# Transposing one input of a channel cross-attention on VectorE instead of TensorE, on one Trainium2 core

## What is computed

```python
rgb, geo = x transposed to (b, n, c), ctx transposed to (b, n, c)
def xca(q, k, v):                       # attention over channels, not positions
    attn = softmax(einsum('bhni,bhnj->bhij', q, k) * scale)
    return einsum('bhnd,bhde->bhne', v, attn)
res_p2r = xca(rgb @ wq_rgb.T, geo @ wk_point.T, geo @ wv_point.T) @ proj_p2r.T
res_r2p = xca(geo @ wq_point.T, rgb @ wk_rgb.T, rgb @ wv_rgb.T) @ proj_r2p.T
out = transpose(rgb + res_p2r) + transpose(geo + res_r2p)
```

## Time and profile before

| | |
|---|---|
| runs of the kernel before | 145.23, 145.45, 145.67 us (median 145.45) |
| profiled execution, span | 144.7 us (no time of its own is given beside the three runs) |
| TensorE matmul busy | 135.4 us, 94% |
| VectorE busy | 99.1 us, 68% |
| ScalarE busy | 92.6 us, 64% |
| GpSimd busy | 2.0 us, 1% |
| DMA | 25.80 MB, mean 178 GB/s |
| mean granted clock of TensorE | 0.985 |

### The profile page before, as it was taken

How to read it: one execution, slowest core, us unless ns; L and a number is a source line. 1 busy time by engine, 2 the same in 40 slices (tenths; PEclk the granted TensorE clock), 3 DMA queues, 4 the chain that set the end, 5 groups by cost and what they waited for, 6 DMA issues and landing times. The chain is left out here.

```text
span 144.7 us, 3130 instructions
## 1 busy us (share of the span) xinstructions
PE 135.4 (94%) x968; PEld 123.4 (85%) x968; DVE 99.1 (68%) x245; ACT 92.6 (64%) x207; POOL 2.0 (1%) x11
## 2 busy tenths in 40 slices
PE   7599889999999999999999999999999999997871
PEld 7399778999999998999999998989999998986560
DVE  0125797678686977777786878777785969777740
ACT  3125948675766767785876767686867677582821
POOL 5000000000000000000000000000000000000000
PEclk9959999999999999999999999999999999999998
DMA  4999243431919467482828475583927730303033
GB/s 132 246 418 417 96 140 150 147 147 31 348 61 248 191 183 249 142 289 60 296 86 263 172 239 196 165 270 89 310 53 245 317 147 0 145 0 150 2 147 145
DMA packets 7642, 25.80 MB, mean 178 GB/s; under 512 B 849, under 2 KB 977, under 8 KB 7633
## 3 DMA queue, kind: packets, MB, share of 16 engines
q1 hardware_dynamic: 7632, 25.69, 52.2%
HBM read 17.30 MB, written 8.39 MB: 178 GB/s over the span
## 5 line engine op out<-in xcount | busy, mean ns | idle before, releaser
L383 DVE COPY gt<-gt_ps 128x512 f32<-128x512 f32 x32 | 22.1, 691 | 18.1 <-PE gt_ps L228 18.1
L238 PE MATMUL gu_ps<-gt,xt 128*128 128x128 f32 x256 | 34.5, 281 | 0.0
L238 PEld LDWEIGHTS gu_ps<-gt,xt 128*128 128x128 f32 x256 | 33.2, 198 | 1.2
L372 ACT COPY out_sb<-out_ps 128x512 f32<-128x512 f32 x32 | 17.7, 587 | 18.0 <-DMA out_dram<-out_sb 11.0
L387 DVE TENSOR_TENSOR x_lo<-x_raw,x_hi 128x1024 fp32r<-128x1024 f32 x16 | 19.6, 1226 | 4.1 <-ACT x_hi L327 4.1
L318 ACT COPY xt<-xt_ps 128x512 f32<-128x512 f32 x32 | 18.9, 589 | 5.0 <-PE xt_ps L228 4.9
L354 ACT ACTIVATE expd<-scores,min_neg 128x128 f32<-128x128 f32 x32 | 12.6, 395 | 12.8 <-DVE min_neg L427 12.8
L228 PE MATMUL xt_ps<-ident,x_raw 128*128 128x128 f32 x128 | 19.3, 273 | 1.1 <-DMA x_raw<-in_x_dram 1.1
L228 PE MATMUL gt_ps<-ident,g_raw 128*128 128x128 f32 x128 | 19.8, 278 | 0.6 <-DMA g_raw<-in_ctx_dram 0.6
L387 DVE TENSOR_TENSOR g_lo<-g_raw,g_hi 128x1024 fp32r<-128x1024 f32 x16 | 19.5, 1216 | 0.0
L228 PEld LDWEIGHTS xt_ps<-ident,x_raw 128*128 128x128 f32 x128 | 15.4, 142 | 3.2 <-DMA x_raw<-in_x_dram 1.3
(11 more groups left out here) (51 smaller groups left out, 193.1 us busy)
## 6 DMA issues: line engine op xcount, KB each, us to landing
x_raw<-in_x_dram SPq DMA_DIRECT2D x15, 512.0 KB, 3.5
g_raw<-in_ctx_dram SPq DMA_DIRECT2D x15, 512.0 KB, 5.3
out_dram<-out_sb SPq DMA_DIRECT2D x15, 512.0 KB, 5.9
x_raw<-in_x_dram SPq DMA_DIRECT2D x2, 256.0 KB, 3.8
g_raw<-in_ctx_dram SPq DMA_DIRECT2D x2, 256.0 KB, 4.4
out_dram<-out_sb SPq DMA_DIRECT2D x2, 256.0 KB, 2.0
w_sb<-in_weights_dram SPq DMA_DIRECT2D x1, 384.0 KB, 7.1
w_sb<-in_weights_dram SPq DMA_DIRECT2D x1, 128.0 KB, 5.0
```

The source lines that it names most:

```text
L238: last = nc.tensor.matmul(gram_ps, xt[:, cols], gt[:, cols], start=(t == 0), stop=(t == TILES - 1))
L372: nc.scalar.copy(out_sb[:, slot % OUT_SLOTS, cols], out_ps[:, cols]).then_inc(half_copied, 1)
L383: nc.vector.tensor_copy(gt[:, cols], gt_ps[:, cols]).then_inc(gt_copied, 1)
```

## The change

- **G is loaded twice.** Beside the plain `g_raw`, a second copy `gz` is loaded with quarters of the channels and of the positions exchanged: `gz[32 q + k, 256 a + m]` is channel 32 a + k at position 256 q + m. It comes in pieces of 1 KB, by four DMAs of 32 partitions each, for two batches at a time; SP issues quarters 0 and 1, ScalarE quarters 2 and 3.
- **VectorE transposes G** in blocks of 32x32 from `gz` straight into `gt` (`turn_half`, two instructions of 128x512 a batch). TensorE no longer transposes G, and `gt_ps` goes.
- **X stays on TensorE**, in chunks of every eighth column, so that its positions stand in the same order as G's. `xt_ps` shrinks to one half; VectorE makes both copies of it, into a double buffer.
- **Low parts on GpSimd.** `x_lo` and `g_lo` are made by GpSimd, not VectorE.
- s, exp, y and t have a PSUM bank each; the exponentials are written to PSUM, t gets the identity added in place, probs is one instruction in place of two.
- **One more stage.** Transposes run in step i, the gram matrix in i+1, the small products with t in i+2, the last product in i+3, its second output copy in i+4. All steps are written out, with no loop. Four output slots in place of two, 56 warm-up matmuls in place of 24, `ident2` made directly.

The core of the diff: the turned load, then in this order GpSimd's loop, SP's, TensorE's transposes, ScalarE's loop and VectorE's turn.

```diff
-WARM = 24
+WARM = 56
+        g_turn = ctx.rearrange("b (a k) (q m) -> q k (b a) m", a=QUADS, q=QUADS)
+        def load_turned(eng, src, dst, done, first, count, quads):
+            pair, at = first // 2 % PAIRS, first % 2
+            for q in quads:
+                into = dst[q * QUAD:(q + 1) * QUAD, pair, at:at + count, :]
+                eng.dma_start(into.rearrange("p e (a m) -> p (e a) m", a=QUADS),
+                              src[q][:, QUADS * first:QUADS * (first + count), :]).then_inc(done, 16)
...
+            for b in range(B):
+                split_lo(b, x_raw, x_hi, x_lo, x_hi_ready)
+                split_lo(b, g_raw, g_hi, g_lo, g_hi_ready)
...
+            for i in range(2, B + 4):
+                if i % 2 == 0 and i + 2 < B:
+                    sp.wait_ge(gt_turned, 2 * i)
+                    load_turned(sp, g_turn, gz, gz_loaded[(i + 2) // 2 % PAIRS], i + 2, 2, (0, 1))
+                if 0 <= i - 4 < B - 1:
+                    store(i - 4)
+                if i >= 3 and i + 1 < B:
+                    sp.wait_ge(xt_done, 2 * (i - 3) + 2)
+                    sp.wait_ge(lo_ready, 2 * (i - 3) + 2)
+                    load_plain(i + 1)
...
+            def transpose_half(b, half):
+                slot = b % SLOTS
+                pe.wait_ge(x_loaded[slot], 16 * (b // SLOTS) + 16)
+                if 2 * b + half >= 1:
+                    pe.wait_ge(xt_copied, 2 * b + half)
+                blocks = x_raw[:, slot, :].rearrange("p (n j) -> p j n", j=TILES)
+                for t in range(TILES // 2):
+                    last = nc.tensor.transpose(xt_ps[:, t * TILE:(t + 1) * TILE], blocks[:, half * TILES // 2 + t, :],
+                                               ident[:, :])
+                last.then_inc(xt_done, 1)
...
+            for i in range(1, B + 4):
+                g, s, l, e = i - 1, i - 2, i - 3, i - 4
...
+                if i % 2 == 0 and i + 2 < B:
+                    act.wait_ge(gt_turned, 2 * i)
+                    load_turned(act, g_turn, gz, gz_loaded[(i + 2) // 2 % PAIRS], i + 2, 2, (2, 3))
+                if out_on:
+                    evacuate(e, 1)
+                if small_on:
+                    act.wait_ge(uv_done, s + 1)
...
+            def turn_half(b, half):
...
+                if b >= 2:
+                    dve.wait_ge(gram_done, b - 1)
+                blocks = gz[:, pair, b % 2, :].rearrange("p (a i j) -> p j a i", a=QUADS, i=QUAD)
+                first = half * TILES // 2
+                cols = slice(half * HALF, (half + 1) * HALF)
+                nc.vector.transpose(gt[:, b % 2, cols].rearrange("p (j a k) -> p j a k", a=QUADS, k=QUAD),
+                                    blocks[:, first:first + TILES // 2, :, :]).then_inc(gt_turned, 1)
```

More of the change, by code:

```diff
@@ L187, in _ @@
[L187 to L191, removed]
+                sp.dma_start(out[b], out_sb[:, b % OUT_SLOTS, :]).then_inc(out_stored[b % OUT_SLOTS], 16)
@@ L195, in _ @@
+            sp.dma_start(g_raw[:, 1, :], ctx[1]).then_inc(g_loaded[1], 16)
             for b in range(2, SLOTS):
[L196 to L199, removed]
+                load_plain(b)
+            for i in range(2, B + 4):
[8 more added lines that the diff above has]
+                    load_plain(i + 1)
@@ L215, in _ @@
                 nc.tensor.matmul(out_ps[:, 0:P], warm[:, :], warm[:, :], start=True, stop=True)
[L216 to L222, removed]
-                if i_min >= 1:
-                    pe.wait_ge(copied, 2 * i - 1 + half)
+            pe.wait_ge(ident_ready, 3)
@@ L239, in gram_half, with last_parts @@
                 if half == 1:
                     last.then_inc(gram_done, 1)
-            def last_half(b, slot, half, b_min):
+            def last_parts(b, half, first, end):
+                slot = b % SLOTS
                 cols = slice(half * HALF, (half + 1) * HALF)
-                if b_min >= 1:
-                    pe.wait_ge(half_copied, 2 * b - 1 + half)
                 parts = [(t_hi, 0, x_hi), (t_hi, 0, x_lo), (t_hi, 1, g_hi), (t_hi, 1, g_lo), (t_lo, 0, x_hi), (t_lo, 1, g_hi)]
-                for n, (w, which, moving) in enumerate(parts):
+                if first == 0 and b >= 1:
+                    pe.wait_ge(half_copied, 2 * (b - 1) + 1 + half)
+                for n in range(first, end):
+                    w, which, moving = parts[n]
@@ L248, in last_half @@
                     if half == 0 and n == 4:
                         pe.wait_ge(t_lo_ready, b + 1)
-                    last = nc.tensor.matmul(out_ps[:, cols], w[:, which, :], moving[:, slot, cols],
-                                            start=(n == 0), stop=(n == len(parts) - 1))
-                last.then_inc(half_done, 1)
-            def step(i, slot, visit, i_min):
-                gram_on, small_on, last_on = i_min < B, 1 <= i_min <= B, i_min >= 2
-                before = (slot - 2) % SLOTS
-                if gram_on:
-                    turn(i, visit, i_min, 0, x_raw, slot, x_first_loaded, x_loaded, xt_ps, xt_done, xt_copied)
-                    turn(i, visit, i_min, 0, g_raw, slot, g_first_loaded, g_loaded, gt_ps, gt_done, gt_copied)
+                    last = nc.tensor.matmul(out_ps[:, cols], w[:, which, :], moving[:, slot, cols], start=(n == 0),
+                                            stop=(n == len(parts) - 1))
@@ L260, in step @@
+                if end == len(parts):
+                    last.then_inc(half_done, 1)
+            for i in range(B + 3):
+                g, s, l = i - 1, i - 2, i - 3
+                turn_on, gram_on, small_on, last_on = i < B, 0 <= g < B, 0 <= s < B, 0 <= l < B
                 if small_on:
-                    pe.wait_ge(gram_lo_ready, i)
-                    if i_min == 1:
+                    pe.wait_ge(gram_lo_ready, s + 1)
+                    if s == 0:
                         pe.wait_ge(wu_lo_ready, 1)
@@ L306, in step @@
                 if last_on:
-                    last_half(i - 2, before, 1, i_min - 2)
-            steps(pe, step, 0, B + 1)
+                    last_parts(l, 1, 2, 6)
+                if small_on:
+                    pe.wait_ge(y_copied, s + 1)
+                    if s >= 1:
+                        pe.wait_ge(t_lo_ready, s)
+                    nc.tensor.matmul(t_ps[:, 0:P], y_sb[:, 1, :], w_sb[:, PR, :], start=True, stop=True)
+                    nc.tensor.matmul(t_ps[:, P:2 * P], y_sb[:, 0, :], w_sb[:, PP, :], start=True,
+                                     stop=True).then_inc(t_done, 1)
```

348 lines of the change are left out of this document (164 added, 184 removed).

## The result

| | before | changed |
|---|---|---|
| runs, median (us) | 145.56 (145.23 to 146.64, 4 runs) | 158.06 (157.44 to 159.18, 4 runs) |
| ratio, 95% interval | | 1.0835, 1.0777 to 1.0893 |
| profiled span (us) | 144.7 | 156.7 |
| first uv, second uv start (us) | 11.92, 17.71 | 17.33, 29.94 |
| from second uv to span's end (us) | 127.0 | 126.8 |

The change makes the kernel 8% slower; the forecast of 145.2 us was wrong, and so was the range, which ended at 153. The last row of the table says where to look: everything from the second batch's uv on takes as long as before (14 steps are 1.1 us longer, the end behind the last uv is 1.3 us shorter), and the whole loss, 12.2 us, lies in front of it.

The account below looks back on a forecast made before the run. TensorE's list of work was taken to set the step. 13.5 + 6.9 + 100.1 + 3.75 + 7.15 + 5.6 + 7.5 gave a 144.5 us span, plus 0.75 the forecast 145.2, no change; range 139.5 to 153.

Parts of the forecast that it names:

- Head and tail: Start and end of the kernel: uv of batch 0 at 13.5 us, 6.9 for step 2, 7.15, 5.6 and 7.5 for steps 16 to 18.
- Rival D: X loads at even steps: X lands 1.2 us late in six steps behind turned G and a store, 152 us; chance 0.13.
- TensorE's work: TensorE's step of 8.09 us: G's transposes go, 0.83 us a batch, leaving 7.26; 13.3 us could be gained over 16 batches.
- rival B: X's transposes on TensorE: strided weight loads take double, 0.42 us more per four, +8 to 153.2 us; chance 0.13.
- rival A: ScalarE's issues do not hold it, 140.7 us; with the step's gaps of 0.51 hidden as well, 134; chance 0.30.
- Wait 1: TensorE's s waits for ScalarE's uv copy, starting 1.20 us after uv instead of 0.87: gap of 0.31 us a step.
- wait 2: TensorE's y waits for probs, behind VectorE's second X copy: gap of 0.25 us a step.
- Wait 3: ScalarE at even steps: two DMA issues, taken at 0.75 us, delay the uv copy, so s starts 0.75 us later.
- Rival C: VectorE's turn reads at half rate because of the stride, 0.53 us longer each, 149 us; chance 0.10.
- What is hidden: VectorE's step falls to 5.1 of 7.7 us; GpSimd's subtractions, 1.6 to 3.2 us each, are costed at nothing.
- Tail: End of the kernel: step 16 takes 7.15 us, step 17 5.6 and step 18, to the span's end, 7.5.

Follow-up runs that it names:

- the last version: Changed kernel with TensorE's G for batches 0 and 1, X and G first, later ScalarE issues, s behind first gram half, t behind next uv: 136.59 us.

## Why the prediction was wrong

Its own sum against the profile, in us of span:

| term | forecast | measured |
|---|---|---|
| uv of batch 0 | 13.5 | 17.33 |
| step 2, to uv of batch 1 | 6.9 | 12.61 |
| 13 full steps | 103.85 | 106.7 |
| step 16 to the end | 20.25 | 20.07 |
| span | 144.5 | 156.7 |

**The step that failed is "Head and tail": 13.5 and 6.9.** Both were summed from TensorE's and VectorE's instructions, with every tile in place when wanted. When X of batches 1 and 2 would land was never asked, though all of it was at hand: SP's order in the kernel, the sizes, and 330 GB/s in the start. By those, 4.5 MB ahead and 0.5 MB of its own would have put X of batch 2 at 15 us or later, past the 14.0 us at which its transposes were to begin (13.5 and uv's 0.45). That names the wait, but only the first 1 to 2 of its 8 us: the trace shows 22.40, for the rate was 290, hardly a byte moved in the first 2 us, and 5.8 MB had moved by the landing (257 GB/s over 22.4 us), so that later loads shared the rate. 9.5 of the 12.2 us missed lie here, and the earlier landing in one experiment, the shorter queue in another, gave 3.9 and 6.4 us back (156.7 to 152.8 and 150.3). Of the first two rows of the table only the sum holds from one execution to the next. Uv of batch 0 is late by X of batch 1 (2.18 us of waiting) and by gram halves at half clock behind that wait (1.91 us in place of 1.06); in the runs that leave the start's loads alone it comes at 14.4 to 17.3 us, and uv of batch 1 at 28.0 to 29.9 all the same, since X of batch 2 lands at 20.8 to 22.5.

**Rival D was the right mechanism in the wrong place.** It was worked out for even steps, where the changed kernel shows no wait for X: its slow steps cover the late load. Freed of ScalarE's issues, the kernel shows it at once (five waits of 1.1 to 2.5 us in odd steps); and its remedy is the order alone, since 277 to 308 GB/s were carried with X on time. That the pieces of 1 KB cost rate is not excluded: the start ran at 286 to 294 GB/s against 330 before, and at 338 (3 to 14 us) in the run that loads no turned G for batches 0 and 1, but no run tells their size from the other differences there.

**TensorE's work was right.** 7.26 us of work in a step; 7.22 in the last version. Four transposes of strided X take 0.45 from start to start (92.86 to 93.31) where four took 0.40 to 0.44, so a strided load costs 0.01 us at most and not 0.11, and B was to count from 0.03 on: **rival B is false.** (Their weight loads are recorded as 0.19 us long, 0.14 before; the contiguous loads of the gram matrix are 0.19 as well, and only the distance of starts tells a cost.) Of rival A one figure does not follow: its hidden gaps are 0.56 by waits 1 and 2, or 0.44 by the step of 7.7, and not 0.51.

**Wait 1 and wait 2 were right.** s starts 1.07 us after uv in odd steps (1.20 forecast), and an odd step takes 7.75 (7.7 forecast), of which 0.28 went when s had a gram half ahead of it, and 0.25 more when y and t got more work ahead of them.

**Wait 3 was right in kind and too small.** Forecast 0.75 us more in an even step, measured 1.18: two issues on ScalarE take 0.87, not 0.75, and the turn ahead of them ends 0.4 us later, since it takes 1.151 and not 0.69. With five such steps that is 2.1 of the 2.8 us in the third row; the other 0.7 are thirteen steps of 7.75 in place of 7.70. **Rival C is true**, with its 0.45 us a turn near the 0.53 assumed; the run with adjacent elements shows it. The Trainium skill's rule (Advanced Engine Details and Errata, SBUF Cachelines) that fewer than two hits on a line of 16 bytes cost rate agrees with VectorE's 1.151 against 0.703; for TensorE's weight loads, to which the prediction applied it as well, the trace does not show it.

**What is hidden** was half right. GpSimd took 2.38 us a subtraction, within the bounds of 1.6 and 3.2, and in the changed kernel's full steps nobody is seen to wait for it; the estimate of 2.4 from the Trainium skill (GPSIMD Engine Reference, Performance versus the Vector engine) agrees. But "I cost it at nothing" named a step of slack, and not who waits behind it on SP: put into the old kernel, it cost 4.8%, of which 3.3 points went when the store no longer stood behind the reload.

**Tail**: 20.07 against 20.25.

## What to carry to other kernels

When a change adds loads, write down for each early load what stands ahead of it in all queues, in bytes, and divide by the rate that the start shows: that landing time, not the engines' work, may set the first steps. Here the sum would have been too early by some 7 us and would still have shown the wait. In a tight pipeline a wait that is taken away uncovers the next (issues, then late X, then the copy of uv); single edits then look worthless, and have to be tried together before the idea is given up. A low result on the whole says little of a part: the same idea measured +8.4% as first written and -6.4% with five further edits, most of them of order.

## What was not expected of the hardware

- A stride of 32 bytes costs VectorE's block transpose 64% (1.151 against 0.703 us for 128x512), TensorE's transposes at most 0.05 us in four.
- Issuing a DMA is not free on ScalarE: 0.43 us each in the steady part. On SP, where X and G took 0.35 and 0.43 at 20 us, the issue of X at 8.71, in the crowded start, took 2.15.
- With low parts on GpSimd in the old kernel, one VectorE subtraction of 128x256 between two SBUF tiles (t_lo) took 1.91 us at 139.52, while a GpSimd subtraction ran (138.81 to 141.14), against 0.42 at 126.71, where none ran:

```profile
138.81 2.33 POOL L170 TENSOR_TENSOR g_lo<-g_raw,g_hi 128x1024 fp32r<-128x1024 f32 x1
139.52 1.91 DVE L425 TENSOR_TENSOR t_lo<-t_sb,t_hi 128x256 fp32r<-128x256 f32 x1
```

In the changed kernel, which reads one input from PSUM, the mean of all 16 is 0.42. In the two runs of this kind t_lo met a GpSimd subtraction six times: each time it took 0.97 to 1.91 us and ended 0.27 to 0.29 us behind it, as if held until its end, and the mean of 16 rose to 0.583. It was not tested apart; in the run with the store first the end waits for `g_lo` and not for this.
